# Order of the first transfers, two input semaphores, two memsets and the selection casts in a two-layer kernel

## What is computed

```python
x = x + L0_ffn(L0_cond(x, cond_64))      # two mixtures of experts
x = x + L1_ffn(L1_cond(x, mask, ...))    # attention, then a mixture of experts
# the first block, L0_cond:
logits = (x @ wt.T + repeat(cond_64 @ wg.T, 32)) / 2
scores = softmax(logits); keep the two largest of 8, divide by their sum
gp = leaky(x @ w_gate[e]); up = x @ w_up[e]
y = sum_e weight[e] * ((gp * up) @ w_down[e]) + shared expert
```

## Time and profile before

| | us |
|---|---|
| median of 3 runs (265.47 to 266.8) | 266.52 |
| the profiled execution | 268.66 |
| its span | 266.9 |
| TensorE busy | 247.8 (93%) |
| VectorE busy | 214.8 (80%) |
| ScalarE busy | 147.5 (55%) |
| GpSimd busy | 106.1 (40%) |

### The profile page before, as it was taken

How to read it: one execution, slowest core, us unless ns; L and a number is a source line. 1 busy time by engine, 2 the same in 40 slices (tenths; PEclk the granted TensorE clock), 3 DMA queues, 4 the chain that set the end, 5 groups by cost and what they waited for, 6 DMA issues and landing times.

```text
span 266.9 us, 5111 instructions
## 1 busy us (share of the span) xinstructions
PE 247.8 (93%) x1848; PEld 198.0 (74%) x1848; DVE 214.8 (80%) x423; ACT 147.5 (55%) x239; POOL 106.1 (40%) x145
## 2 busy tenths in 40 slices
PE   7898999889999969978999998989899999999994
PEld 5675557667899949967767766768688888888884
DVE  5997768987876497886559987889998888788883
ACT  2655524336631455788235455387687767877550
POOL 2799410133592746844337676533140101101000
PEclk9999999999999999999689999999999999999999
DMA  6994430010300002201300000007192000000002
GB/s 169 236 275 55 140 138 0 1 42 0 52 2 0 2 5 79 75 6 31 92 2 4 2 4 0 2 4 234 37 306 95 0 0 2 1 0 0 2 0 81
DMA packets 25178, 14.54 MB, mean 54 GB/s; under 512 B 11969, under 2 KB 21862, under 8 KB 25153
## 3 DMA queue, kind: packets, MB, share of 16 engines
q1 hardware_dynamic: 24608, 13.92, 19.1%
q0 software_dynamic: 544, 0.29, 0.9%
HBM read 13.58 MB, written 0.62 MB: 53 GB/s over the span
## 4 chain that ended last, share of the span: by engine, by line
PE 58%; DVE 22%; POOL 9%; issue 4%; ACT 3%; DMA 2%; SPq 1%; DVEq 0%; POOLq 0%; ACTq 0%
PE ps L924 13%; PE ps L925 12%; PE ps L926 12%; PE ps L1082 5%; PE ps L1021 3%; POOL w_lo L503 3%; PE ps L1048 3%; PE ps L985 2%; DMA w_stage<-in_L_cond_w_up 2%; DVE arena L1671 2%; DVE arena L1689 1%; DVE g_lo L1761 1%; PE ps L1137 1%; DVE ssum L1664 1%; DVE arena L1654 1%
## 5 line engine op out<-in xcount | busy, mean ns | idle before, releaser
L924 PE MATMUL ps<-act_hi,w_hi 128*128 128x512 f32 x120 | 48.3, 403 | 3.6 <-DVE arena L1394 2.2
L865 ACT ACTIVATE att_bias<-ps,bias 128x512 f32<-128x512 f32 x64 | 43.5, 689 | 13.2 <-PE ps L926 11.3
L925 PE MATMUL ps<-act_lo,w_hi 128*128 128x512 f32 x120 | 47.1, 393 | 0.0
L926 PE MATMUL ps<-act_hi,w_lo 128*128 128x512 f32 x120 | 47.0, 392 | 0.0
L1761 DVE TENSOR_TENSOR g_lo<-att_bias,g_hi 128x1024 fp32r<-128x1024 f32 x32 | 39.9, 1258 | 0.7
L924 PEld LDWEIGHTS ps<-act_hi,w_hi 128*128 128x128 f32 x120 | 22.5, 188 | 10.1 <-issue 5.2
L926 PEld LDWEIGHTS ps<-act_hi,w_lo 128*128 128x128 f32 x120 | 22.6, 188 | 5.0
L925 PEld LDWEIGHTS ps<-act_lo,w_hi 128*128 128x128 f32 x120 | 22.6, 188 | 4.5
L1757 DVE CAST g_hi<-att_bias 128x1024 fp32r<-128x1024 f32 x16 | 12.4, 774 | 8.6 <-ACT att_bias L865 8.6
L704 ACT ACTIVATE xc<-ps 128x512 f32<-128x512 f32 x18 | 10.8, 598 | 14.8 <-PE ps L926 14.8
L1444 DVE TENSOR_TENSOR arena<-arena,ps 128x512 f32<-128x512 f32 x24 | 16.1, 684 | 3.4 <-PE ps L985 3.3
(11 more groups left out here) (281 smaller groups left out, 581.4 us busy)
## 6 DMA issues: line engine op xcount, KB each, us to landing
arena<-gate_m SPq DMA_DIRECT2D x16, 256.0 KB, 4.7
w_stage<-in_L_ffn_W SPq DMA_DIRECT2D x9, 256.0 KB, 2.8
w_stage<-in_L_ffn_W SPq DMA_DIRECT2D x1, 1792.0 KB, 7.9
x_tok<-in_x SPq DMA_DIRECT2D x2, 256.0 KB, 3.3
w_stage<-in_L_ffn_w_gate SPq DMA_DIRECT2D x1, 512.0 KB, 4.7
w_stage<-in_L_ffn_w_up SPq DMA_DIRECT2D x1, 512.0 KB, 6.2
w_stage<-in_L_cond_Wq SPq DMA_DIRECT2D x1, 512.0 KB, 5.6
f_down<-in_L_ffn_w_down SPq DMA_DIRECT2D x1, 512.0 KB, 5.7
```

What stands on the lines that cost most here:

```text
L865: act.activation(gelu[:, k % 2, b, :], bank(b), ACT.Gelu, bias=bias1[:, c:c + 1])\
L924: pe.matmul(dst, wh, xh, start=first, stop=False)
L925: pe.matmul(dst, wh, xl, start=False, stop=False)
L926: return pe.matmul(dst, wl, xh, start=False, stop=last)
```

## The change

The three small transfers are issued behind w_gate and w_up of L0_cond. x has a semaphore for each half, and TensorE waits for each half just ahead of its transposes. The memsets of gate_sel and gate_rows_r go from VectorE to GpSimd, behind `ident`, with a semaphore `pool_sel` for gate_sel. The two casts go from behind cond_rows to the first place behind `ident`, with a wait for `pool_sel`.

```diff
--- before.py
+++ after.py
@@ -231,7 +231,7 @@
 
 
         ld = {n: sem("ld_" + n) for n in (
-            "x", "small", "vec", "wc", "wcs", "wf", "wq", "cd", "fd", "wo", "kv", "gk", "rp", "att", "null",
+            "x0", "x1", "small", "vec", "wc", "wcs", "wf", "wq", "cd", "fd", "wo", "kv", "gk", "rp", "att", "null",
             "bias_w", "bias_r", "w1", "w1_last",
             "gate_mw", "out")}
         w2_in = [sem(f"ld_w2_{e}") for e in range(M_EXP)]
@@ -279,6 +279,7 @@
         pe_rows = sem("pe_rows")
         pe_gate = sem("pe_gate")
         v_sel = sem("v_sel")
+        pool_sel = sem("pool_sel")
         v_warm = sem("v_warm")
         v_gates = sem("v_gates")
         pool_w2 = sem("pool_w2")
@@ -348,10 +349,7 @@
             for s in range(HALVES):
                 sp.dma_start(x_tok[:, s * HT:(s + 1) * HT, :],
                              a["x"].rearrange("b s c -> (b s) c").rearrange("(t p) c -> p t c", p=P)
-                             [:, s * HT:(s + 1) * HT, :]).then_inc(ld["x"], 16)
-            sp.dma_start(wt_rows[:, :], a["L0_cond_wt"]).then_inc(ld["small"], 16)
-            sp.dma_start(small_rows[0:SEQ, :], a["cond_64"]).then_inc(ld["small"], 16)
-            sp.dma_start(small_rows[SEQ:SEQ + C_EXP, :], a["L0_cond_wg"]).then_inc(ld["small"], 16)
+                             [:, s * HT:(s + 1) * HT, :]).then_inc(ld[f"x{s}"], 16)
             cview = w_stage[:, C0:C0 + 2 * C_BLK * P].rearrange("p (g c) -> p g c", g=2)
             fview = w_stage[:, F0:F0 + 2 * F_BLK * P].rearrange("p (g c) -> p g c", g=2)
             for view, pre, n, s, shared in ((cview, "L0_cond_", C_PAIRS, "wc", "wcs"),
@@ -359,6 +357,10 @@
                 for g, name in enumerate(("gate", "up")):
                     sp.dma_start(view[:, g, 0:n * P].rearrange("p (e m) -> p e m", m=DH),
                                  a[pre + "w_" + name].rearrange("e h m -> h e m")).then_inc(ld[s], 16)
+                if s == "wc":
+                    sp.dma_start(wt_rows[:, :], a["L0_cond_wt"]).then_inc(ld["small"], 16)
+                    sp.dma_start(small_rows[0:SEQ, :], a["cond_64"]).then_inc(ld["small"], 16)
+                    sp.dma_start(small_rows[SEQ:SEQ + C_EXP, :], a["L0_cond_wg"]).then_inc(ld["small"], 16)
                 for g, name in enumerate(("gate", "up")):
                     sp.dma_start(view[:, g, n * P:(n + 1) * P], a[pre + "sw_" + name]).then_inc(ld[shared], 16)
             sp.dma_start(c_down[:, 0:C_PAIRS, :], a["L0_cond_w_down"].rearrange("(q e) m c -> (e m) q c", e=2))\
@@ -461,6 +463,8 @@
             pool.affine_select(out=ident[:, :], in_=ident[:, :], compare_op=ALU.not_equal, fill=1.0, base=0,
                                pattern=[[-1, P]], channel_multiplier=1).then_inc(ready, 1)
 
+            pool.memset(gate_sel[:, :, :].bitcast(f32), 0.0).then_inc(pool_sel, 1)
+            link(pool.memset(gate_rows_r[:, :].bitcast(f32), 0.0))
             link(pool.memset(gk[:, :], 0.0))
             link(pool.memset(router_w[:, :], 0.0))
             pool.memset(tiny[:, :], 1e-20)
@@ -932,8 +936,8 @@
             for _ in range(8):
                 pe.matmul(bank(3), w2b_hi[:, 0:P], w2b_hi[:, :], start=True, stop=True)
             pe.wait_ge(ready, 1)
-            pe.wait_ge(ld["x"], 32)
             for s in range(HALVES):
+                pe.wait_ge(ld[f"x{s}"], 16)
                 for t in range(HT):
                     mm = pe.transpose(bank(4 + s)[:, t * P:(t + 1) * P], x_tok[:, s * HT + t, :], ident[:, :])
                 mm.then_inc(pe_xT, 1)
@@ -1353,9 +1357,12 @@
             link(dve.memset(eps[:, :], LN_EPS))
             link(dve.memset(wt_T[:, :], 0.0))
             dve.memset(vec[:, :], 0.0)
-            dve.memset(gate_rows_r[:, :].bitcast(f32), 0.0)
-            link(dve.memset(gate_sel[:, :, :].bitcast(f32), 0.0))
             dve.wait_ge(ready, 1)
+            dve.wait_ge(pool_sel, 1)
+            for g in (0, LOW_ROW):
+                dve.tensor_copy(gate_sel[g:g + F_EXP, :, :].rearrange("p q (h m) -> p (q h) m", h=2),
+                                ident[g:g + F_EXP, g:g + F_EXP].unsqueeze(2).broadcast_to([F_EXP, F_EXP, DH]))\
+                    .then_inc(v_sel, 1)
             dve.tensor_reduce(seq_tile[:, :], ident[0:SEQ, 0:SEQ].rearrange("p (t q) -> p t q", q=BPT), AX, ALU.add)
             link(dve.tensor_reduce(seq_slot[:, :], ident[0:SEQ, 0:SEQ].rearrange("p (t q) -> p q t", q=BPT), AX,
                                    ALU.add))
@@ -1381,11 +1388,6 @@
                               bank(7)[0:SEQ, 128:128 + C_EXP].unsqueeze(1).broadcast_to([SEQ, TILES, C_EXP]),
                               seq_tile[:, :].unsqueeze(2).broadcast_to([SEQ, TILES, C_EXP]), ALU.mult)\
                 .then_inc(v_small, 1)
-            for g in (0, LOW_ROW):
-                dve.tensor_copy(gate_sel[g:g + F_EXP, :, :].rearrange("p q (h m) -> p (q h) m", h=2),
-                                ident[g:g + F_EXP, g:g + F_EXP].unsqueeze(2).broadcast_to([F_EXP, F_EXP, DH]))\
-                    .then_inc(v_sel, 1)
-
             def c_unit(u):
 
                 s, b = divmod(u, C_BLK)
```

## The result

| | before | after |
|---|---|---|
| median of 12 runs | 266.56 us | 271.17 us |
| lowest and highest | 265.39 to 269.89 | 268.08 to 275.56 |
| profiled execution, its span | 268.66, 266.9 | 268.75, 267.0 |

The change made the kernel slower: 1.0113 of the time before (95% interval 1.0076 to 1.015), about 3 us, and 4.6 us by the medians. The prediction, 266.4 us with a range of 265.2 to 267.8, missed. Every ratio here leaves out executions more than 1.5% above the fastest of their kernel as disturbed (5 of the changed kernel's 12, at mean clocks of 0.956 to 0.981); the medians keep them, because here, as the experiments show, low clocks follow the kernel.

The account below looks back on a forecast made before the run. VectorE's order of work, the routing chain with c_units between, was taken to bound the opening. A 0.45 us later chain less 0.5 us of collisions, kept as -0.1 us, gave a 266.4 us median, range 265.2 to 267.8.

Parts of the forecast that it names:

- the page's chain: Opening: GpSimd's low halves lead into line 985; if right, 0.38 us gained, 266.1 us; no chance of its own.
- The hole in the queue: SyncE's queue: long slots behind large transfers delay wg's issue to about 5.1 us instead of 2.65; chance 0.48.
- The casts cost nothing: VectorE's opening: moved casts end at 4.85 us, before the copy at 5.83; without that cover 0.5 us at most.
- the 0.5 I took: Opening: fewer VectorE collisions with GpSimd's low halves return 0 to 0.9 us; 0.5 taken, the excess of line 1368.
- GpSimd's memsets and the input halves: Opening: memsets, 1.9 us, fit GpSimd's idle 4.83 us; x on two semaphores gains nothing, as transposes start without idle time.
- Then line 998 ends near 9.43 + 1.4 = 10.85: TensorE's opening: small transfers taken 1.4 us later, so line 1406 starts near 10.95 us, 0.45 later.
- my sum: Opening: 0.45 us lost by the later routing chain, 0.5 returned from collisions; about zero, kept as -0.1 us.
- I take a shift of c_unit(5) to pass one to one to the end: After the opening: TensorE goes on without a pause of its own clock time, so c_unit(5)'s shift reaches the end whole.
- the sign I had set: Line 985 moving by over 0.5 us without the end following would show the passing on of the shift wrong.
- The slower one: Small transfers wait behind 512 KiB of weights, wg lands at 9.8 us, everything behind 1.9 late: 268.4 us; chance 0.12.
- The one with the small loads hardly late and the collisions gone: Opening: full 1.0 us from the casts plus 0.7 us of collisions, 1.7 us gained, about 264.8 us; chance 0.12.
- The first rival: SyncE's queue not held: wg issued at 3.6 us, line 1406 0.2 to 0.6 earlier, about 265.9 us; chance 0.28.

Follow-up runs that it names:

- e1: The changed kernel with the three small transfers back ahead of the weights; median 267.14 us, 0.9995 of before.
- e11: The kernel before with only the memsets and casts moved, one semaphore for x, old transfer order; median 268.01 us, 1.0011 of before.
- Group two: Five unread TensorE products ahead of the first `values`, near 127 us; alone on the kernel before, median 265.39 us, 0.9943 of before.
- e10: The changed kernel with small transfers back ahead of the weights, plus five unread products ahead of the first `values`; median 265.99 us, 0.9962 of before.
- Group one: Six unread TensorE products ahead of the second turning of normed tiles, near 99 us; with Group two on the kernel before, 268.27 us.
- e2: The kernel before with only the order of the transfers changed; median 272.6 us, 1.0052 of before.
- e5: The kernel before, old transfer order, with TensorE waiting idle ahead of wt for three GpSimd memsets; median 275.96 us over 6 runs.
- e3: The changed kernel with five more warm-up products ahead of TensorE's wait for the small transfers; median 267.41 us, 1.0046 of before.

## Why the prediction was wrong

**What held.** VectorE's routing chain bounds the opening and not GpSimd's low halves, which the page's chain named: the halves started 0.3 us earlier and line 985 1.33 us later, in step with c_unit(5) (1.32). The shift then passed on unchanged, at 96 us still 1.3. The hole in the queue is real: wg issued at 5.37 us (I had 5.1), TensorE takes the small transfers at 7.47 (7.6); but I had a slot over 0.8 us on both w_up and wt, and w_up's took 0.61, wt's 1.57. From issue to landing wg took 2.05 us by the chain of waits, just under my 2.1 to 2.8. The roughly 2 us that the prediction cites from the Trainium skill (DMA: Bandwidth & Descriptors, Anatomy of one DMA) stand there for transfers that GpSimd issues; this one, SyncE's, agrees with them. The casts cost nothing in their new place (over at 4.51, I had 4.85). Yet by the rows they seem to have collided with GpSimd there, which I had ruled out by their 1.2 us: the first took 1.32 us and ended 0.5 us behind GpSimd's memset of gate_rows_r (2.31 to 3.26 us), the second took 0.68, and GpSimd's next two memsets took 0.60 and 0.66 us, before 0.17 and 0.18:

```profile
3.32 0.60 POOL L468 MEMSET gk<- 128x96 f32 x1
3.98 0.66 POOL L469 MEMSET router_w<- 128x96 f32 x1
```

The 1.2 us of before had been taken beside the low halves. Of the collisions behind the chain's start, line 1368's second run fell to 0.69 us, line 1409 to 0.23 and line 1427 to 0.38; they return 0.55, 0.35 and 0.40 us. But line 1425 grew from 0.22 to 0.74, and in all the chain, 1.87 us late at its start, is 1.32 late at c_unit(5): 0.55 returned, close to the 0.5 I took, though not by line 1368 alone. That is partly luck. GpSimd's memsets and the input halves are worth nothing, as costed.

**What failed, first step.** "Then line 998 ends near 9.43 + 1.4 = 10.85". That sum carries TensorE's durations over an idle time of 1.4 us. The wait itself was right, the 2.02 us behind it were not: the logits took 3.63 at 1.2 GHz, line 1002 starts at 11.91, and the chain starts at 12.38 us instead of 10.95. In the terms of my sum, +0.45 - 0.5, the first was off by 1.4 us and the second by almost nothing: measured +1.87 - 0.55 = +1.32 us.

**What failed, second step.** "I take a shift of c_unit(5) to pass one to one to the end", and the median taken as the profiled time less 2.1 us. By the sign I had set, line 985 moves by over 0.5 us and the end does not follow (spans of 266.9 and 267.0 us), the passing on was wrong. The shift does pass until half clock takes a different share of the two executions, but it is the smaller half. A kernel's executions differ by how often TensorE's clock falls, and I had read the granted clock of one execution as a property of the kernel. That one had two stretches where 27 of 35 have one. The range had no term for the number of stretches, though the page showed the 0.6 in its PEclk line; each costs some 1.8 us (before: 266.3, 268.4, 269.3, 271.6 us for one to four). That the profiled execution after took 268.75 us where I had forecast about 268.6 is luck: both profiles happen to have two.

**The rivals.** The slower one ended on the right side by the wrong mechanism: wg landed near 7.4 us, not 9.8. It named the right place and the wrong price. The one with the small loads hardly late and the collisions gone has its opening in e1: it is 1.7 us earlier there (line 1406 at 9.37, and line 1435 at 22.75 against 24.43). But the collisions are not gone in e1: line 1368's second run took 1.24 us as before and line 1409 0.77 instead of 0.58; only line 1427 fell, from 0.78 to 0.17. Over all executions the time is that of before, because of further stretches. The first rival, the queue not held, is refuted by wg's issue at 5.37 us.

**Open.** Why e1 and e11 have four stretches in 9 of 24 executions isn't settled. Group two takes them down to two at most (e10), so they seem to hang on the idle time near 127 us; but that is 1.3 us in the profiled executions of e1, e11 and the kernel before alike. No profile caught an execution with four, so where these lie isn't shown, nor where the changed kernel's lie beyond the two in its profile. Group one at a better place was not tried.

## What to carry to other kernels

A transfer that is small but first in TensorE's order should not be queued behind large ones, even when these are what the next stage seems to wait for. When a change leaves TensorE idle, cost the work behind the gap at both clock levels, and look for other idle stretches that lie near the edge. Compare executions by their mean granted clock before comparing spans; where a wait can't be removed, products that nobody reads kept the clock here, where they had nothing to wait for themselves.

## What the runs showed of the hardware

- Behind an idle time of 1.37 us the changed kernel ran at half clock for 3.4 us, behind 1.50 us e2 for 10.2 us, behind 0.96 us e5 for 6.8 us. Yet the kernel before has one of 1.36 us ahead of unit 2 and kept 1.00 there. Near 99 us both kernels have the same idle time, 1.68 and 1.67 us: the one kept 1.00 behind it, the other fell. The Trainium skill (TensorE: Matmul & The Clock Gate, HAM oscillation) warns that idle gaps put TensorE back to its slow level; the trace agrees on that. The gaps it speaks of are far longer than these, and there the measurement decides: the length of the gap alone doesn't tell, and the same program falls in some executions and not in others.
- The profile gives the granted clock of the first microseconds as 1.00, but the durations tell of a slow start: in the kernel before the warm-up products begin 0.42 us apart from 2.48 us on, the same form 0.23 us apart at 10 us. It doesn't end at a fixed time: the 8 transposes of x take 1.06 us in the changed kernel and 1.91 in e3, at the same start of 5.03. TensorE takes wt without a wait at 6.06 us in e1 and at 6.62 in e11, so that alone can move the opening by 0.6 us.
- SyncE's slot on a transfer behind large ones can be long: 1.57 us on wt, whose 4 KB are not the reason. My estimate that it lasts until 1,100 to 1,350 short runs are left over put wg's issue within 0.3 us, but foretold a long slot on w_up that wasn't there.
